# Last cross attention and last mixture of a decoder on one Trainium2 core: closing chain set one step to a slot, first route and up products placed from slot 88 on

## The reference, cut to what matters

```python
x = x + _L2_xattn_ref(_layernorm(x), ctx_1024, ctx_1024, w_concat)        # 16 heads of 8, softmax(q k / sqrt(8)) v
x = x + _L2_ffn_ref(_layernorm(x), w_gate, w_up, w_down)                  # fp4 quantised: silu(gate) * up, then down, 352 wide
x = x + _L3_attn_ref(_layernorm(x), queries)                              # (h Q^T) (h^T h), no softmax
x = x + _L3_xattn_ref(_layernorm(x), ctx_1024, ctx_1024, mask, 0, ...)    # linear attention, residual and a layer norm of its own
x = x + _L3_ffn_ref(_layernorm(x), router_w, w1, b1, w2, b2)              # 8 experts, top 2, gelu, 512 wide
```

## Time and profile before

| | us |
|---|---|
| median of 3 runs | 1251.13 (1246.38 to 1257.37) |
| the profiled execution | 1246.21 |
| its span, first to last instruction | 1244.7 |
| TensorE busy | 1014.1 |
| VectorE busy | 811.4 |
| ScalarE busy | 611.7 |

### The profile page before, as it was taken

How to read it: one execution, slowest core, us unless ns; L and a number is a source line. 1 busy time by engine, 2 the same in 40 slices (tenths; PEclk the granted TensorE clock), 3 DMA queues, 4 the chain that set the end, 5 groups by cost and what they waited for, 6 DMA issues and landing times.

```text
span 1244.7 us, 19906 instructions
## 1 busy us (share of the span) xinstructions
PE 1014.1 (81%) x7630; PEld 548.4 (44%) x7649; DVE 811.4 (65%) x2024; ACT 611.7 (49%) x1018; POOL 241.2 (19%) x305
## 2 busy tenths in 40 slices
PE   5777679998999965667576889999758878769999
PEld 4233223333677652334353233466412333336757
DVE  7786867741324477888867884477688787665412
ACT  2556346666334427777753777423115556423342
POOL 2833300000000223674542000000222000000000
PEclk9789879999899995677767999999858889889999
DMA  8333040000000310238012500800100300100000
GB/s 302 95 78 79 30 176 2 2 2 1 1 1 1 90 46 1 82 123 149 6 38 71 176 2 2 141 1 1 52 14 28 115 1 2 34 1 1 1 9 9
DMA packets 34785, 61.23 MB, mean 49 GB/s; under 512 B 4771, under 2 KB 25076, under 8 KB 33092
## 3 DMA queue, kind: packets, MB, share of 16 engines
q1 hardware_dynamic: 33828, 58.64, 16.7%
q10 hardware_dynamic: 864, 1.33, 0.3%
HBM read 42.91 MB, written 16.65 MB: 48 GB/s over the span
## 4 chain that ended last, share of the span: by engine, by line
PE 57%; DVE 30%; ACT 5%; issue 4%; DMA 1%; POOL 1%; SPq 0%; DVEq 0%; ACTq 0%; POOLq 0%
PE ps_e L865 9%; PE ps_s L875 9%; PE ps_v L668 6%; DVE mx L1841 6%; PE ps_e L604 5%; PE ps_s L625 3%; PE ps_e L602 3%; DVE ps_s L1837 2%; PE ps_e L969 2%; ACT work L1382 2%; DVE mx L1831 2%; PE ps_s L956 2%; DVE work L2320 2%; DVE work L2322 2%; DVE xn L1797 2%
## 5 line engine op out<-in xcount | busy, mean ns | idle before, releaser
L1382 ACT ACTIVATE work<-ps_e 128x512 f32<-128x512 f32 x448 | 250.7, 598 | 140.1 <-PE ps_e L604 135.3
L2595 POOL TENSOR_TENSOR rstd<-rstd,halves 128x2 f32<-128x2 f32 x52 | 36.6, 704 | 694.9 <-DVE rstd L1784 694.7
L1841 DVE TENSOR_REDUCE mx<-ps_s 128x2 f32<-128x1024 f32 x128 | 153.9, 1222 | 25.6 <-PE ps_s L625 24.3
L625 PE MATMUL ps_s<-ctx_stack,q_stack 49*128 49x512 bf16 (+1 forms) x384 | 127.5, 452 | 45.1 <-DVE mx L1841 32.2
L604 PE MATMUL ps_e<-q_stack,ctx_stack 52*128 52x256 bf16 (+1 forms) x768 | 149.2, 291 | 17.2 <-issue 6.4
L1484 ACT ACTIVATE work<-ps_s,keep 128x512 f32<-128x512 f32 x136 | 93.0, 687 | 137.0 <-PE ps_s L875 134.0
L668 PE MATMUL ps_v<-work,vaug 128*32 128x256 f32 x1536 | 127.8, 408 | 4.5 <-ACT work L1370 4.3
L865 PEld LDWEIGHTS ps_e<-ffn_w,work 128*128 128x128 f32 x960 | 118.2, 196 | 21.1 <-issue 19.9
L865 PE MATMUL ps_e<-ffn_w,work 128*128 128x128 f32 x960 | 120.0, 280 | 0.8 <-DVE x L2031 0.8
L875 PE MATMUL ps_s<-xnT,ffn_w 128*128 128x512 f32 x240 | 115.6, 605 | 4.2 <-ACT work L1484 4.2
L2041 DVE SCALAR_TENSOR_TENSOR x<-ps_e,gates,x 128x128 f32<-128x128 f32 x128 | 38.9, 346 | 120.7 <-PE ps_e L865 117.7
(11 more groups left out here) (379 smaller groups left out, 1803.8 us busy)
## 6 DMA issues: line engine op xcount, KB each, us to landing
q_stack<-q_scr SPq DMA_DIRECT2D x32, 192.0 KB
ffn_w<-in_L0f_w SPq DMA_DIRECT2D x1, 4608.0 KB, 14.5
ffn_w<-in_L1f_w SPq DMA_DIRECT2D x1, 3456.0 KB, 13.1
q_scr<-parts SPq DMA_DIRECT2D x16, 192.0 KB, 2.1
c_scr<-ffn_w SPq DMA_DIRECT2D x12, 256.0 KB, 7.7
kx_scr<-ffn_w SPq DMA_DIRECT2D x12, 256.0 KB, 3.3
ctx_stack<-kx_scr SPq DMA_DIRECT2D x2, 1536.0 KB
ctx_stack<-c_scr SPq DMA_DIRECT2D x2, 1536.0 KB
```

The source lines that it names most:

```text
L625: return pe.matmul(ps_s[i][:, parity, :], q_stack[p0:p0 + n_rows, b, pair, part * P:(part + 1) * P], ctx_stack[p0:p0 + n_rows, pair, b * S ...
L1382: act.activation(pt[:, parity, :, :].rearrange("p k q -> p (k q)"), bank[f"e{parity}"], ACT.Exp).then_inc(exped, 1)
L1841: m = dve.tensor_reduce(mx[:, b, :, pair, part], ps_s[i][:], AX, ALU.max, negate=True)
```

## The change

A table `STEP_AT` maps each step of the chain to a new offset: 4 to 12 stay, then the gaps close: 15 to 13, 16 to 14, 17 to 15, 18 to 16, 20 to 17, 21 and 22 to 18, 24 to 19, 25 to 20, 27 to 21, and one by one up to 37 to 31. This holds for all four batches. The orders of norms, turns and PSUM tiles follow. With the last offset 31, batch 1's chain ends in slot 87, so `TAIL0` becomes 88: the route of group 0 stands in slot 88, and slots 88 to 92 of the attention's closing run inside `l3_tail`, on the one tile. `PIECES_BEFORE` gives one piece to each slot from 89 to 117 (two, gate and bias, in 93), again 30 pieces. The chain's last slot is 118 on TensorE instead of 124. What is computed, and by which instructions, stays the same. In the text, "old" numbers are the steps' names in the code; the others are the new offsets.

```diff
--- before.py
+++ after.py
@@ -130,16 +130,24 @@
     return {p: i + 1 for i, p in enumerate(pairs)}
 
 
+STEP_AT = {4: 4, 5: 5, 7: 7, 8: 8, 9: 9, 10: 10, 11: 11, 12: 12, 15: 13, 16: 14, 17: 15, 18: 16, 20: 17, 21: 18,
+           22: 18, 24: 19, 25: 20, 27: 21, 28: 22, 29: 23, 30: 24, 31: 25, 32: 26, 33: 27, 34: 28, 35: 29, 36: 30, 37: 31}
 CHAIN = [("L2f", 3), ("L3a", 17), ("L3x", 24), ("L3x-inner", 33), ("L3f", 34)]
-tail = sorted((close_slot(X2, b) + at, b, st) for st, at in CHAIN for b in range(B))
-tail = [(st, b) for _, b, st in tail]
+
+
+def chain_slot(b, at):
+    return close_slot(X2, b) + STEP_AT.get(at, at)
+
+
+tail = sorted((chain_slot(b, at), st != "L2f", b, at, st) for st, at in CHAIN for b in range(B))
+tail = [(st, b) for _, _, b, _, st in tail]
 L2_ORDER = [("L2a", 0), ("L2a", 1), ("L2x", 0), ("L2x", 1), ("L2a", 2), ("L2x", 2), ("L2a", 3), ("L2x", 3)]
 front = [(st, b) for st in ORDER[:6] for b in range(B)] + L2_ORDER
 VAR_AT = order_of(front + tail)
 NORM_AT = order_of(front + [p for p in tail if p[0] != "L3x-inner"])
 TURNS = [("L2f", 7), ("L3a", 20), ("L3x", 27), ("L3f", 36)]
-turned_tail = sorted((close_slot(X2, b) + at, b, st) for st, at in TURNS for b in range(B))
-TURN_AT = order_of(front + [(st, b) for _, b, st in turned_tail])
+turned_tail = sorted((chain_slot(b, at), b, at, st) for st, at in TURNS for b in range(B))
+TURN_AT = order_of(front + [(st, b) for _, b, _, st in turned_tail])
 BEFORE = {"L2f": "L2x", "L3a": "L2f", "L3x": "L3a", "L3f": "L3x"}
 X_AT = order_of([(st, b) for st in ("L0a", "L0x", "L1a", "L1x", "L2a") for b in range(B)]
                 + [(BEFORE[st], b) for st, b in tail if st in BEFORE])
@@ -148,8 +156,8 @@
 PROJ_AT = order_of([("L1x", b) for b in range(B)] + [("L3x", b) for b in range(B)])
 
 CHAIN_PS = [17, 20, 22, 24, 33]
-PS_AT = order_of([(at, b) for _, b, at in sorted((close_slot(X2, b) + at, b, at) for at in CHAIN_PS for b in range(B))])
-LAST = {A0: 54, X0: 96, X1: 96, X2: 93, "chain": 125}
+PS_AT = order_of([(at, b) for _, b, at in sorted((chain_slot(b, at), b, at) for at in CHAIN_PS for b in range(B))])
+LAST = {A0: 54, X0: 96, X1: 96, X2: 93, "chain": 119}
 CFILL = {X0: 32, X1: 128, X2: 192}
 PLACED = 2
 Q_ROW = 24
@@ -217,7 +225,7 @@
 L1F_UNITS = 2 * (NE + 1)
 SWIGLU_FIRST = [(u, j) for u in range(3) for j in range(F1J)]
 SWIGLU_BEFORE = {88: 1, 89: 1, 90: 1, 91: 1, 92: 1, 93: 1}
-TAIL0 = 94
+TAIL0 = 88
 PIECES = [("up", u, k) for u in range(3) for k in range(2)] + [("gate", 0, 0), ("bias", 0, 0)]
 PIECES[4:8] = PIECES[6:8] + PIECES[4:6]
 for u in range(NE):
@@ -226,8 +234,7 @@
             PIECES.append(("up", u + 2, k))
         PIECES.append(("down", u, k))
 ROUTE1 = len(PIECES) - 2
-PIECES_BEFORE = {95: 2, 96: 1, 97: 1, 98: 1, 99: 2, 101: 1, 102: 1, 103: 1, 104: 1, 105: 1, 106: 1, 107: 1, 108: 1, 109: 1,
-                 110: 1, 111: 1, 113: 1, 114: 2, 116: 1, 117: 1, 118: 1, 120: 1, 122: 2, 123: 2, 124: 1}
+PIECES_BEFORE = {t: 2 if t == 93 else 1 for t in range(89, 118)}
 L3F_OWN = 6
 
 
@@ -485,7 +492,9 @@
 
     def chain_steps(slot):
         for b in range(B):
-            yield b, slot - close_slot(X2, b)
+            for at in STEP_AT:
+                if chain_slot(b, at) == slot:
+                    yield b, at
 
     def route_tmp(i):
         flat = parts[:].rearrange("p s t -> p (s t)").bitcast(F32)
@@ -935,6 +944,8 @@
                 for i in range(n, n + PIECES_BEFORE.get(t, 0)):
                     l3_piece(0, i)
                 n += PIECES_BEFORE.get(t, 0)
+                if t < LAST[X2]:
+                    cross_slot(X2, t, kp("L2x_T"), None, window_tile)
                 chain(t)
             for i in range(n, len(PIECES)):
                 if i == ROUTE1:
@@ -1522,6 +1533,8 @@
                     l3_piece(0, i)
                 n += PIECES_BEFORE.get(t, 0)
                 chain(t, False)
+                if t < LAST[X2]:
+                    cross_slot(X2, t, None)
                 chain(t, True)
             l3_route(1)
             for i in range(len(PIECES)):
@@ -2093,6 +2106,8 @@
                 for i in range(n, n + PIECES_BEFORE.get(t, 0)):
                     l3_piece(0, i)
                 n += PIECES_BEFORE.get(t, 0)
+                if t < LAST[X2]:
+                    cross_slot(X2, t, "L2f", window_tile)
                 chain(t)
             for i in range(n, len(PIECES)):
                 if i == ROUTE1:
```

## The result

The changed kernel takes 1268.88 us (median of 4 runs, 1264.69 to 1273.1) against 1250.47 (1246.38 to 1257.37) for the kernel before on the same chip: a ratio of 1.0142, with an interval of 1.0109 to 1.0176. It is 18.4 us slower. The forecast of 1263.8 fell 5 us short. It was summed on the span of the profiled run, though, and there it is 12.5 short: 1257.4 forecast, 1269.9 measured.

What follows compares the result with a forecast made beforehand. TensorE, busy 81% of the span, was taken as the bound, waiting for VectorE's chain. (d) -0.5, holding (a) to (c), (e) +3.2 and (f) +10.0 gave +12.7 us, on the median 1263.8; range 1244 to 1273.

Steps and rivals of the forecast that it cites:

- the likeliest case: The forecast itself, +12.7 us to a median of 1263.8; own range 1259 to 1268, chance 0.38.
- the first rival: Clock falls at each new wait (slots 69, 101, 118), about 2 us each: +18.7 in all, 1269.8; chance 0.15.
- (d): Slots 81 to 88, second period: first route product at about 1098.4 against 1098.86, -0.5 us (bounds -9.4, +3).
- (e): At the route: turns, weighted sums and other products formerly done before it now come behind, +3.2 us (2.4 to 3.7).
- (f): Slots 88 to 118, inside the mixture: waits sum to 17.9 us against 7.9 idle before, +10.0 (+3 to +13).
- (b): Slots 66 to 69: VectorE's quantisation shares slots with another batch's inner norm; new 7.2 us wait before the transposes (0 to 7.2).
- (a): Slots 53 to 63: three more batch 0 steps among the row maxima on VectorE, +1.6 us (0 to 2.6).
- (c): Slots 73 to 79: old waits before the post-norm turn go, small ones appear, net -2.0 us (-3 to 0).
- the rule: Skill's HAM oscillation: gaps between product bursts halve the clock, so waits of slots 69 and 101 would cost more than themselves.
- The falling clock: Products after waits of slots 69, 101 and 118 run at the lower clock: +6, 1269.8 in all; chance 0.15.
- The waits only change place: Rival: queues have more slack than the slot walk shows, small waits overlap; +5 us, 1256; chance 0.29.
- VectorE gets ahead, and the hole fills: Rival: VectorE finishes within TensorE's cover, waits of slots 69, 85, 101, 118 go; -7.0 us, 1244.1, or -13; chance 0.18.

Runs made afterwards that it cites:

- e4: Changed kernel plus 7, 8 and 5 unread products ahead of the fp4 hidden-row transposes of batches 1, 2 and 3: 1260.9 us, ratio 1.0103.
- e12: Changed kernel with the fills of e4 and the moved pieces of e5, VectorE's order as changed: 1253.94 us, ratio 1.0020.
- e5: Changed kernel with two moves: one up product between gates and bias, two pieces placed in slot 118: 1256.08 us, ratio 1.0058.
- e10: e8 without any useless product, keeping the gap, moved bias and two pieces in slot 120: 1250.92 us, ratio 1.0024.
- e1: Changed kernel's compressed chain alone, route back in slot 94 and pieces as before (slot 96's moved to 97): 1270.94 us, ratio 1.0189.
- e2: Changed kernel with VectorE doing steps 11 and 12 of the next batch ahead of steps 27 and 28: 1265.31 us, ratio 1.0154.
- e3: Changed kernel but two free slots kept between steps 12 and 15, chain closed only behind 18, mixture from slot 90: 1263.74 us, ratio 1.0128.
- e6: Kernel before plus useless products: 2 ahead of batch 1's transposes, 2 and 5 ahead of L3f turns of batches 0 and 1: 1252.51 us, ratio 0.9997.
- e11: e8 with 2 more useless products ahead of the last output projection, slot 90: 1244.21 us, ratio 0.9963.
- e9: Kernel before with the fills of e6 and the order of pieces of e5, as control for e8: 1246.79 us, ratio 0.9977.
- e8: e3 plus 13 useless products ahead of transposes and turns, bias one piece later, two pieces in slot 120: 1244.06 us, ratio 0.9945.

## Why the prediction was near, and where it failed

I gave 0.53 to "within 1%" and 0.37 to "slower"; it is slower by 1.4%, with the whole interval above 1%. The time is within the range of 1244 to 1273, but just outside the likeliest case's own 1259 to 1268, and nearest to the first rival, that the clock falls at every new wait (1269.8), to which I had given 0.15. That the time fell so near has luck in it. By marks of the two profiles the steps below fell short by 6.6 us (d), 4.8 (e) and 1.1 (f), 12.5 in all, as much again as the forecast of 12.7. The medians show only 5 of them, mainly because before's profile lies under its median and after's above.

**The waits of this table were right to within 0.6 us; the one at step 21 was not.** What the forecast had, and what the timeline of after shows (us):

| | forecast | measured |
|---|---|---|
| (b) steps 9 to 12 with 27 and 28 on VectorE | 13.5 | 14.17 |
| (b) wait, slot 69 | 7.2 | 6.92 |
| (f) turn of slot 88, `turn_close`, `project_out` | 1.4, 1.1, 1.1 | 1.68, 1.05, 1.14 |
| (f) tile `s1`, bias, bank m, step 9 | 0.45, 2.8, 0.6, 1.7 | 0.52, 3.33, 0.71, 1.66 |
| (f) wait, slot 101 | 5.5 | 5.47 |
| (f) wait, slot 118 | 3.2 | 3.40 |
| (f) idle between the routes, against before | +10.0 | +11.05 |

Of (a), the first +1.6 us: measured against slot 44, where the changed kernel was 1.86 us ahead, the last row maximum is 2.27 us late. Of (c), the wait of 2.49 us did go; the one at step 21 is 1.46 instead of 0.4. The wait before the second transposes (7.86) had no forecast of its own, only the time of its end.

**Step (d) failed by 6.6 us**: first route at 1105.01, where 1098.4 was forecast. Of these, 1.3 were there at the first transposes (1053.10 for 1051.8) and 3.8 arose up to the second (45.33 us for 41.5). In that interval the clock was at 0.50 to 0.57 for 15 us, behind the wait at step 21; with the fills of e4 it stayed at 1.00 and the interval took 39.65. Of that difference of 5.7 us, 4.9 lie behind that wait, 0.8 between the first transposes and it. The last 1.5 are the transposes at 1.51 and what follows them: the sum had 1.1 us for ScalarE's copies, but TensorE runs two weighted sums (L677) and a turn (L559) at the low clock between its transposes and the down product, 2.6 us of its own queue (1099.88 to 1102.52).

**Step (e) was over-priced and carried a hidden term.** It gave +3.2 us for products left over at the route; the busy time between the routes rose by 8.03. e12 has all of these products, a clock of 0.98 between the routes, 74.66 us busy there, of which 5 fills take about 4.4: 70.3 for the work itself. So the left-over work is near 1.1 us, and the remaining 6.9 of the changed kernel are the low clock. The sentence that failed is the one that follows the rule: "The sum above has no such cost beyond the rows of before".

**The falling clock** was in the text as a rival and priced at about 2 us for each of three waits. It was too small. By e5 and e10, 4.7 us of waits (bias and slot 118) carried 4.9 and 4.7 us of slower products with them. The evidence against it, a clock of 1.00 in 1114 to 1118 with TensorE busy for 1.89 of 4 us, was a wait of 1.91 us. I had generalised from one row. It is not only that most of the new waits are longer (3.3 to 7.9): behind 1.46 us at step 21 the clock fell for 13 us in the changed kernel and in e5, for 10 in e1 and e2, for 3 in e12, and not at all in e4. e4 differs from the changed kernel only in the fills ahead of the transposes, and e12 is equal to e4 there. So the length of a wait alone doesn't tell it; what came ahead counts too, and not even that settles it in every execution. The Trainium skill (TensorE: Matmul & The Clock Gate, section "HAM oscillation") says that gaps between bursts of products bring half the clock for the burst that follows. The trace agrees in that: 3.33 us of wait and then 0.52 in the changed kernel. But not every gap does it: 1.40 us and then 1.00 in e5.

**"The waits only change place" (0.29) fell** as a forecast of the time: the small waits did not overlap, and the bias wait was longer than before (3.33 for 1.91). But as a mechanism it shows where a wait is removed by itself: e2, e3, e6 and e11 each took one away and found part of it or all of it at the next product that needs VectorE or ScalarE.

**"VectorE gets ahead, and the hole fills" (0.18) fell** in the first period already, with 6.92 us of wait. Something of it appears once the clock is held: from the last row maximum to the first route it takes 73.8 us in the changed kernel, 68.1 before, and 63.9 in e12. Its turning point (13.5 us of work against 6 to 8 of cover) was the right quantity.

**What stays open.** After which waits the clock falls: neither their length nor the work ahead sorts all the rows. What the remaining loss of e10 over before (0.24%) consists of; and whether the closed-up chain gains anything over e9. That a fill works through the clock and not otherwise was not tried in another way than by the clock's rows: a fill of another kind of work would tell.

## What to carry to other kernels

When a step of a chain is set closer to the one that feeds it, add up the queue of the engine between them (here 13.5 us on VectorE for some 6 of cover on TensorE), slot by slot and with the work of the other batch that lands in the same slots. The waits so found were right to within 0.6 us here, but for one. Then add a price for the products behind it: in two pairs of kernels 4.7 us of wait cost 9.4 to 9.6 in all. Short waits belong in that sum as well. First move existing work into the wait (two pieces gave 10 to 13 us in each of three kernels), then, if nothing can be moved, keep TensorE busy with products that nobody reads; and look where the next wait is, because the gain ends there.

## What the runs showed of the hardware

Products whose results nobody reads can save time: 13 of them made a kernel 0.79% faster (e8 and e10), since those behind them ran at the upper level. Waits of 1.40 and 1.91 us left the granted clock at 1.00 in the row around them (e5; the earlier trace rows); in the rows around and behind waits of 3.33, 3.45 and 6.92 us it is 0.52, 0.50 and 0.51. But no length divides the two. In before, 1.76 us ahead of 1082.69 stand beside 0.62 in 1082 to 1086. Behind 2.10 us in e11, after a stretch in which TensorE had worked 1.44 of 4 us, it was 0.57. And the same 1.46 us at step 21 were followed by 0.50 to 0.57 for 15 us in the changed kernel and by 1.00 in e4, whose earlier long wait was filled; e12, the same up to there, had 3 us at the lower level.

The start of the stretch moved by more than some of the effects: the last row maximum of slot 63 came between 1027.19 and 1039.04 us in the 14 profiles, most of which have moved steps in slots 53 to 63; in e8 and e11, which are equal up to there, it came at 1031.69 and 1039.04. One profile places and sizes a wait, but doesn't rank two kernels that lie within half a per cent.
